# A recommendation tower on one core: rows of all four groups kept in their own places, gathers without waits, all groups written out

## The reference

```
e = stack([tbl_f[ids[:, f]] for f in range(26)], axis=1)      # 512 x 26 x 64, the gather
x = layer_norm(dense @ Wd.T, gd, bd)                          # 512 x 128
y = layer_norm(einsum('bnd,ed->bne', e, Ws), gs, bs)          # 512 x 26 x 128
y = layer_norm(einsum('bne,pn->bep', y, Wsi), gsi, bsi)       # 26 fields become 32
T = concatenate([x[:, None, :], swapaxes(y, 1, 2)], axis=1)   # 33 vectors of 128 per sample
Z = einsum('bnd,bmd->bnm', T, T)                              # all pair products
z = layer_norm(Z[:, TRIL_I, TRIL_J] @ Wl.T, gl, bl) * mask    # 528 pairs -> 512, first 384 live
h = concatenate([z, dense], axis=1)
h = maximum(h @ W_top1 + b_top1, 0)
h = maximum(h @ W_top2 + b_top2, 0)
y = h @ W_top3                                                # 512 x 1
```

## Time and profile before

| what | value |
|---|---|
| median of 3 runs | 245.53 us (245.27 to 246.01) |
| profiled execution, its own time | 243.04 us |
| its span, first to last instruction | 241.2 us |
| mean granted TensorE clock | 0.83 |
| PE / PEld busy | 173.7 us (72%) / 131.6 us (55%) |
| DVE / ACT / POOL busy | 121.1 / 76.2 / 108.1 us |
| moved by DMA | 8.14 MB, of it 3.41 MB by the gathers' queue |
| chain that ended last | PE 53%, issue 17%, another core or an unknown queue 13%, DVE 9%, ACT 5% |

### The profile page before, as it was taken

The page is one execution under the profiler, slowest core; times in us unless marked ns, Lnnn a source line. Parts: engine busy times, 40 slices in busy tenths (PEclk is TensorE's granted clock), DMA queues, the critical chain, the costliest instruction groups (busy, mean ns, idle before and its releaser), DMA issues.

```text
span 241.2 us, 4708 instructions
## 1 busy us (share of the span) xinstructions
PE 173.7 (72%) x1983; PEld 131.6 (55%) x1983; DVE 121.1 (50%) x225; ACT 76.2 (32%) x158; POOL 108.1 (45%) x110
## 2 busy tenths in 40 slices
PE   0668825649981954689558728979929799867896
PEld 0318721235551724458528518846729686767695
DVE  6474400238958270546482920916863984773012
ACT  2021400026684420515321310414414165350224
POOL 3787777727775173456570660557450000330000
PEclk9985555757996796899875955997967999999999
DMA  6515453101111010010110010011010000000000
GB/s 190 178 24 125 111 155 97 45 5 26 28 22 29 3 30 16 14 22 16 20 26 8 16 24 6 11 24 22 16 27 0 0 0 1 0 3 5 0 3 0
DMA packets 5728, 8.14 MB, mean 34 GB/s; under 512 B 2357, under 2 KB 3279, under 8 KB 5712
## 3 DMA queue, kind: packets, MB, share of 16 engines
q0 software_dynamic: 3328, 3.41, 7.4%
q1 hardware_dynamic: 1664, 3.65, 5.0%
q10 hardware_dynamic: 720, 0.85, 1.2%
HBM read 7.91 MB, written 0.00 MB: 33 GB/s over the span
## 4 chain that ended last, share of the span: by engine, by line
PE 53%; issue 17%; another core or an unknown queue 13%; DVE 9%; ACT 5%; DMA 2%; ACTq 1%; DVEq 0%
PE ps_z L990 8%; PE ps_gq L947 6%; PE ps_y L968 5%; PE ps_ut L958 5%; PE ps_tail L1045 4%; PE ps_tail L1022 3%; PE ps_z L1002 3%; PE ps_tail L899 2%; DVE var L701 2%; DMA gs_sb<-in_gs_row_dram 2%; PE ps_y L1022 2%; PE ps_gq L941 2%; PE ps_tail L931 2%; PE ps_tail L1054 1%
## 5 line engine op out<-in xcount | busy, mean ns | idle before, releaser
L285 POOL DMA_INDIRECT G<-in_table_dram,idx x104 | 104.0, 1000 | 74.9 <-PE ps_ut L958 41.7
L990 PE MATMUL ps_z<-V 128*32 128x34 f32 x1024 | 21.1, 218 | 28.0 <-issue 26.3
L673 DVE TENSOR_TENSOR qg<-ps_gq,G 128x384 f32<-128x384 f32 (+1 forms) x16 | 9.4, 588 | 57.0 <-PE ps_gq L947 23.2
L990 PEld LDWEIGHTS ps_z<-V 128*32 128x32 f32 x1024 | 16.9, 128 | 35.3 <-issue 32.3
L968 PE MATMUL ps_y<-ut,wcg 64*128 64x512 f32 x64 | 21.6, 751 | 7.2 <-issue 7.0
L958 PE MATMUL ps_ut<-S,G 128*128 128x192 f32 (+4 forms) x128 | 25.1, 348 | 2.2 <-DVE G L686 1.5
L947 PE MATMUL ps_gq<-gram,gt 128*128 128x128 f32 x104 | 19.2, 335 | 8.9 <-ACT gt L367 7.7
L958 PEld LDWEIGHTS ps_ut<-S,G 128*128 128x128 f32 x128 | 23.5, 229 | 3.2 <-DVE G L686 2.1
L701 DVE TENSOR_REDUCE var<-sq 128x32 f32<-128x1024 f32 x16 | 19.4, 1213 | 8.5 <-ACT sq L381 7.9
L381 ACT ACTIVATE sq<-V 128x1024 f32<-128x1024 f32 x16 | 16.9, 1058 | 20.3 <-DVE V L696 20.3
L947 PEld LDWEIGHTS ps_gq<-gram,gt 128*128 128x128 f32 x104 | 16.4, 236 | 10.5 <-ACT gt L367 7.8
(11 more groups left out here) (138 smaller groups left out, 228.3 us busy)
## 6 DMA issues: line engine op xcount, KB each, us to landing
G<-in_table_dram,idx POOLq DMA_INDIRECT x104
w1z<-in_w_z_dram SPq DMA_DIRECT2D x1, 768.0 KB
wl<-in_wl_blocks_dram SPq DMA_DIRECT2D x1, 768.0 KB
dns<-in_dense_t_dram ACTq DMA_DIRECT2D x1, 512.0 KB
w1d<-in_w_d_dram SPq DMA_DIRECT2D x1, 512.0 KB
wl<-in_wl_blocks_dram SPq DMA_DIRECT2D x1, 512.0 KB
w2s<-in_w_dram SPq DMA_DIRECT2D x1, 512.0 KB
wrow<-in_wsi_rows_dram SPq DMA_DIRECT2D x1, 208.0 KB
```

What stands on the lines that cost most here:

```text
L285: pool.indirect_dma_start(G[:, j, g, :], None, table, bass.IndirectOffsetOnAxis(ap=idx[:, k:k + 1], axis=0)).then_inc(gathered[c], 16)
L990: mm = pe.matmul(ps_z[32 * qb:32 * qb + 32, bb // 8, col:col + SLOTS], V[:, b, 0:NPROJ], V[:, b, :], start=True, stop=True)
```

## The change

`G` gets a place for every group (26 KB a partition in place of 6.5 KB). GpSimd's wait for `ut_ps` goes. Each batch of each group has a semaphore of its own, 16 in place of 4, and since the group must then be a plain number when the program is built, the three loops are written out (the diff shows TensorE's; VectorE's and ScalarE's are changed alike).

```diff
-        G = sb("G", [P, TILES, 2, D])
+        G = sb("G", [P, NG, TILES, 2, D])
...
-        gathered = [sem(f"gathered{c}") for c in range(NC)]
+        gathered = [[sem(f"gathered{gp}_{c}") for c in range(NC)] for gp in range(NG)]
...
-            sp.wait_ge(gathered[0], 2 * len(batch(0)) * 16)
+            sp.wait_ge(gathered[0][0], 2 * len(batch(0)) * 16)
...
             for gp in range(NG):
                 for c in range(NC):
-                    if gp:
-
-                        pool.wait_ge(ut_ps, nth(gp - 1, c))
                     for j in batch(c):
                         for g in range(2):
...
-                                G[:, j, g, :], None, table,
-                                bass.IndirectOffsetOnAxis(ap=idx[:, k:k + 1], axis=0)).then_inc(gathered[c], 16)
+                                G[:, gp, j, g, :], None, table,
+                                bass.IndirectOffsetOnAxis(ap=idx[:, k:k + 1], axis=0)).then_inc(gathered[gp][c], 16)
...
-            with pe.Fori(1, NG - 1) as gp:
+            for gp in range(1, NG - 1):
                 slots23(gp)
                 slots01(gp + 1)
...
             def transpose_rows(gp, c, first=False):
                 js = batch(c)
-                pe.wait_ge(gathered[c], (gp + 1) * 2 * len(js) * 16)
+                pe.wait_ge(gathered[gp][c], 2 * len(js) * 16)
```

More of the change, by code:

```diff
@@ L262, in _ @@
             for h, (k, end) in enumerate(((0, 2), (2, KB))):
-                sp.wait_ge(gathered[1 + h], 2 * len(batch(1 + h)) * 16)
+                sp.wait_ge(gathered[0][1 + h], 2 * len(batch(1 + h)) * 16)
                 sp.dma_start(wl[:, k:end, :], wl_blocks[:, k:end, :]).then_inc(ld_wl[h], 16)
-            sp.wait_ge(gathered[3], 2 * len(batch(3)) * 16)
+            sp.wait_ge(gathered[0][3], 2 * len(batch(3)) * 16)
             sp.dma_start(w2s[:, :, :], w2).then_inc(ld_w2, 16)
@@ L551, in _ @@
             first_slots01(1)
-            with act.Fori(1, NG - 1) as gp:
+            for gp in range(1, NG - 1):
                 slots23(gp)
@@ L673, in variance1 @@
                 dve.tensor_tensor(qg[:, 0:n * P], ps_gq[:, 0:n * P],
-                                  G[:, js[0]:js[0] + n, :, :].rearrange("p j g d -> p (j g d)"),
+                                  G[:, gp, js[0]:js[0] + n, :, :].rearrange("p j g d -> p (j g d)"),
                                   ALU.mult).then_inc(q_used, 1)
@@ L684, in scale_rows @@
                 dve.wait_ge(r1_ready, nth(gp, c))
-                rows = G[:, js[0]:js[0] + n // 2, :, :].rearrange("p j g d -> p (j g) d")
+                rows = G[:, gp, js[0]:js[0] + n // 2, :, :].rearrange("p j g d -> p (j g) d")
                 dve.tensor_tensor(rows, rows, r1[:, 0:n].unsqueeze(2).broadcast_to([P, n, D]), ALU.mult).then_inc(g_scaled, 1)
@@ L862, in _ @@
             first_slots01(1)
-            with dve.Fori(1, NG - 1) as gp:
+            for gp in range(1, NG - 1):
                 slots23(gp)
@@ L940, in transpose_rows @@
                 for n, j in enumerate(js):
-                    mm = pe.transpose(ps_gq[:, n * P:(n + 1) * P], G[:, j, :, :].rearrange("p g d -> p (g d)"), eye[:, :])
+                    mm = pe.transpose(ps_gq[:, n * P:(n + 1) * P], G[:, gp, j, :, :].rearrange("p g d -> p (g d)"), eye[:, :])
                 mm.then_inc(gt_ps, 1)
@@ L957, in project_fields @@
                         begins = (P * j // NF) // CB != chunk or (P * j) % (CB * NF) == 0
-                        mm = pe.matmul(ps_ut[:, chunk % 2, col:col + n], G[:, j, :, :].rearrange("p g d -> p (g d)"),
+                        mm = pe.matmul(ps_ut[:, chunk % 2, col:col + n], G[:, gp, j, :, :].rearrange("p g d -> p (g d)"),
                                        S[:, j, :, :].rearrange("p s q -> p (s q)")[:, scol:scol + n],
```

## The result

The changed kernel takes 288.42 us (median of 4 runs, 288.12 to 288.66) against 245.4 us before (median of 4) on the same kind of chip: ratio 1.178, 95% interval 1.168 to 1.188. Forecast were 268 us, with a range up to 278: the direction was right, and the size was missed by half, 43 us in place of 23. Later runs added something larger: on other chips of the same type the kernel before takes 188 us, and there the changed one takes 185.

A forecast was written before the change was run, and what follows sets the result against it. TensorE was taken as bound by running gathers holding back its completed work. Held until 140.2 us, plus 125.3 for the rest, made 265.5 of span, 267.3 with 1.84 added, and 268 us with 1 more; range 246 to 278, likeliest 258 to 278.

The forecast's parts named there:

- The gathers are the cause, and the removed wait is what let TensorE run: Running gathers hold back TensorE's completed work; pauses forced by GpSimd's waits for `ut_ps` let it run dense; 268 us, 9% slower.
- Gathers in one piece to 138.9: GpSimd issues all 104 gathers unbroken from 3.67 us, at 1.000 + 0.30 us each, 135.2 us in all.
- TensorE held at 2.3 records per us: From 49.3 to 140.2 us TensorE gets 209 records through, then stands where before it stood at 81.7; chance 0.64.
- its bounds, 0.9 to 5: TensorE's pace beside gathers: 0.9 records per us gives 271 us, up to 278; 3.5 gives 263, 5 gives 245.
- The first hold: First stretch of gathers before the change: 16 TensorE records took from 29.13 until 46.60 us to be done for VectorE.
- the end flat below 3.9 per us: Total time hardly depends on TensorE's pace beside gathers up to 3.9 records per us, and falls fast beyond.
- TensorE free 1.4 us after the last gather: TensorE's hold ends at about 140.2 us, 1.4 after the gathers end, as at 180.68 against 179.31 before.
- The rest, 125.3 us from 81.7: Work after the hold: 159.5 us before, less 34.2 of stalls and late releases with no gathers beside them any more.
- The pile of finished work: TensorE's completed work that can build up beside gathers before a stall shows: some 50 records, or 40 from two windows.
- Loops written out, nothing: Writing out the three loops gains under 1 us; more program to bring in costs nothing to 2 us; taken as nothing.
- No growing hold: Rival: TensorE's trickle ends by itself after some 8 us of a slow call; 230 us, faster; chance 0.13.
- Milder: Rival: TensorE held at a pace of 4 to 5 records per us, 245 to 263 us; 244 to 258 given chance 0.17.

The follow-up runs named there:

- The run with one wait: The changed kernel with one single GpSimd wait for `ut_ps` put back, before group 1's batch 1, the other 64 gathers unbroken: 281.07 us, ratio 1.152.

## Why the prediction was wrong

- *The gathers are the cause, and the removed wait is what let TensorE run.* Right, and against the plain reading that the wait costs nothing. Putting it back gives 244.33 us, leaving the later gathers out 190.83, and plain transfers in their place 191.22.
- *Gathers in one piece to 138.9.* Right: to 136.64, a mean of 0.977 us in place of 1.000.
- *TensorE held at 2.3 records per us.* This step failed, and with it its bounds, 0.9 to 5. Measured are 33 records in 87.7 us, 0.38 per us, six times slower. 2.3 came from stalls of 4 to 9 us, and I carried it over to a run of 91 us. The run with one wait shows what is wrong with that: the pace starts near there, with 18 records in the first 11.1 us after the burst (1.6 per us), and falls to one record in 2.80 us. The first hold, which gave 0.9, was the longest in the trace and already the slowest; I used it as an outer bound where its lesson was the trend. I also called the end flat below 3.9 per us. It is flat only down to 75 records in 90.9 us, 0.8 per us; slower than that, TensorE doesn't get through the dense work ahead of the first pair products, and each record that stays behind costs its time. At 150.67 TensorE stood about where before it stood at 60, not at 81.7 at 140.2: 21.5 us of work more, of which 8.2 is the first call's stall that then doesn't come, so 13.3.
- *TensorE free 1.4 us after the last gather.* Failed too, and again a figure of short runs was used for a long one: 14 us (136.64 to 150.67), 10.5 more than forecast with the gathers' own 2.3 earlier counted in. The short runs of the earlier trace rows lift in 1.4 to 1.9 us, the long one in 14. That one wait after a long run behaves as one after a short run was a premise of the sum that no row showed.
- *The rest, 125.3 us from 81.7.* Right. Moved back to 60 by the same sum it is 125.3 + 13.3 = 138.6; measured from 150.67 to 286.5 are 135.8. The removed stalls came back nowhere: all calls are single bursts but for the 0.63 us named above, which the free chips show as well (0.71 with plain transfers).
- The sum, in span: 265.5 + 10.5 (later release) + 13.3 (more work behind it) - 2.8 (the rest) = 286.5. The pile of finished work is sized once at some 50 records and once at 40 in the prediction; the working gives 40, and no term uses it.
- *Loops written out, nothing.* Right: 0.996 (0.986 to 1.006). The Trainium skill's preference for unrolling (Runtime: NRT & Kernel Launch, Instruction fetch mechanics) would have foretold a gain; up to 3.3 us are inside the interval, and no run shows one.
- *The rivals.* "No growing hold" is true of the free chips, where the change is 1.6% faster. On a holding chip the hold grows. "Milder" lay on the wrong side. No rival was harsher than the forecast; the only slower pace that I worked out was 0.9 per us, though nothing in the profile bounded the pace from below.
- *What I took for the kernel's is the chip's.* The trace spoke of 30 us and more in which TensorE stood for no shown reason. That this could differ between chips was in no case of mine.

Open is what the hold is. The traces place it nowhere: the waits read remote or issue. It came with indirect gathers alone, deepens with a run of them at a 1.25 us period, is much weaker at 1.65 (on one chip), and is all but absent on three of seven chips. TensorE's and GpSimd's results come out late, while the gathers' bytes go on at 23 to 30 GB/s to the end of the run. What it is in an indirect gather (its 0.94 us on GpSimd, its reading of row numbers, its scattered rows) no run took apart. I can't say whether the chip itself or something beside it (how its executions are recorded, say) makes the two kinds; no run here was without the recording. By the Trainium skill (NOTIFIC — the notification-queue block, Overflow: three behaviours, one of which stalls the engine) the pipeline inside the block that takes the engines' trace records pushes back rather than lose one, and can so throttle an engine. That could give such a picture; no run here shows it.

## What to carry to other kernels

A stall that ends with another engine's work, again and again, points to a dependence, also where no wait shows it, and leaving that work out tests it; a semaphore that "nobody needs" may be the pause that keeps it short. A rate read from short stalls isn't the rate of a long one: look at how it runs inside the longest one in the trace before multiplying it, and let the slow side be open. Before a cost is ascribed to a kernel, see the kernel before on a second chip, and before a null result is believed, see in the profile that the experiment changed what it was to change.

## What the runs showed of the hardware that was not expected

- The same program takes 244 us on some chips and 188 on others, and the same change is 1.178 and 0.984. On a free chip the calls beside indirect gathers still take 1.66 to 1.92 us against 1.30.
- Beside an unbroken run of indirect gathers TensorE's trickle is quantised: spacings of 0.70, 1.40, 2.10 and 2.80 us, up and down again.
- GpSimd's own semaphores are late beside them as well: 19 waits of a memset for the memset before it, 12.9 us in all, on a holding chip, and 0.1 us at most on free ones.
- A GpSimd memset of 128 x 1 between gathers costs 0.12 us busy and, on free chips, nothing in period; 128 x 512 costs 0.54 and 0.40, and 128 x 1024 (on a free chip) 0.96 busy for a period of 2.08 us.
- GpSimd's plain transfers of 128 rows take 0.70 us by the profile but 41.3 for 78, since they overlap.
